# Another order of the same instructions in a fused attention kernel, and a load moved behind a transfer

## The reference

```python
# layer 0, per batch (c = 128 channels, n = 512 positions)
energy    = (w_qk y)^T (w_qk x)                    # 512 x 512
attention = softmax(energy, rows)
attention = attention / (1e-7 + attention.sum(over rows))
x_r = relu(w_t (x - (w_v x + b_v) attention) + b_t)
x2  = x + x_r
# layer 1, per batch: 128 rows of 512, 32 query heads on 8 key heads of width 16
q, k, v = x2 Wq + bq, y Wk + bk, y Wv + bv
out = softmax(q k^T / 4 + mask) v Wo + bo
out_x = layernorm(out + x2) * gamma + beta
```

## Time and profile before

| | |
|---|---|
| median of 3 runs | 779.62 us (779.21 to 782.26) |
| the profiled execution | 782.72 us, span 780.3 us |
| mean granted clock of TensorE | 0.980 |
| TensorE busy | 716.9 us (92%), weight loads 579.4 (74%) |
| VectorE busy | 608.3 us (78%) |
| GpSimd busy | 582.2 us (75%) |
| ScalarE busy | 463.5 us (59%) |
| HBM | 41.50 MB read, 8.39 MB written |

### The profile page before, as it was taken

One profiled execution on the slowest core, in us unless ns is written; L12 is line 12 of the kernel. 1 busy time (PEld: TensorE's weight loads), 2 busy tenths in 40 slices (PEclk: granted clock), 3 DMA queues, 4 the chain that ended last, 5 costly groups with the idle time before them and its releaser, 6 DMA issues.

```text
span 780.3 us, 17141 instructions
## 1 busy us (share of the span) xinstructions
PE 716.9 (92%) x4886; PEld 579.4 (74%) x4886; DVE 608.3 (78%) x1030; ACT 463.5 (59%) x1058; POOL 582.2 (75%) x752
## 2 busy tenths in 40 slices
PE   6798979999999999999999999999999999998773
PEld 5676867888788787878778787877878787775642
DVE  5675875969789796969879696978879697885747
ACT  5655638376574937657483855747385665748161
POOL 4886488697877969787896978789697878858054
PEclk9999999999999999999999999999999999999896
DMA  8544361634527262452717254362715436251511
GB/s 321 176 123 125 92 177 55 177 99 148 138 94 191 83 179 89 152 142 89 205 68 184 88 157 129 101 191 74 200 66 171 122 116 170 81 146 61 136 37 61
DMA packets 60363, 101.64 MB, mean 130 GB/s; under 512 B 10032, under 2 KB 30128, under 8 KB 60208
## 3 DMA queue, kind: packets, MB, share of 16 engines
q1 hardware_dynamic: 59616, 101.03, 43.6%
q10 hardware_dynamic: 720, 0.27, 0.2%
HBM read 41.50 MB, written 8.39 MB: 64 GB/s over the span
## 4 chain that ended last, share of the span: by engine, by line
PE 66%; DVE 12%; DMA 9%; issue 5%; SPq 3%; POOL 2%; ACT 1%; DVEq 1%; POOLq 0%; ACTq 0%
PE banks L924 8%; PE banks L840 7%; DMA qstack<-mrep 7%; DVE maxima L1567 6%; PE banks L937 5%; PE banks L871 4%; PE banks L873 4%; PE banks L872 4%; PE banks L895 4%; PE banks L827 2%; PE banks L825 2%; PE banks L826 2%; PE banks L813 2%; SPq L403 2%; PE banks L949 2%
## 5 line engine op out<-in xcount | busy, mean ns | idle before, releaser
L1567 DVE TENSOR_REDUCE maxima<-banks 128x4 f32<-128x512 f32 x256 | 158.9, 685 | 5.9 <-PE banks L895 4.5
L1226 ACT ACTIVATE prob<-banks 128x512 f32<-128x512 f32 x256 | 135.1, 608 | 26.3 <-PE banks L924 25.0
L1592 DVE RECIPROCAL dens<-dens 128x512 f32<-128x512 f32 x30 | 100.4, 3348 | 46.6 <-DMA dens<-sides 46.6
L601 POOL TENSOR_TENSOR ta<-ta,cb_s 128x516 f32<-128x516 f32 x64 | 77.1, 1205 | 74.9 <-ACT ta L1168 74.8
L840 PEld LDWEIGHTS banks<-ta,att 128*128 128x128 f32 x1024 | 119.0, 190 | 2.7 <-POOL ta L608 0.2
L840 PE MATMUL banks<-ta,att 128*128 128x130 f32 x1024 | 119.4, 275 | 0.0
L1160 ACT ACTIVATE att<-banks,negmax 128x512 f32<-128x512 f32 x128 | 88.7, 716 | 33.7 <-DVE negmax L1517 33.6
L1210 ACT ACTIVATE qh<-banks,bq_s 128x256 fp32r<-128x256 f32 x64 | 30.7, 480 | 104.1 <-PE banks L873 104.1
L924 PE MATMUL banks<-qstack,kstack 128*128 128x512 f32 x256 | 81.4, 422 | 9.5 <-DMA qstack<-mrep 9.2
L1517 DVE TENSOR_REDUCE negmax<-banks 128x1 f32<-128x512 f32 x128 | 85.2, 685 | 3.9 <-PE banks L827 3.7
L871 PE MATMUL banks<-x2h,wq_h 128*128 128x256 f32 x256 | 74.5, 291 | 4.1 <-POOL x2l L669 4.1
(11 more groups left out here) (170 smaller groups left out, 1956.1 us busy)
## 6 DMA issues: line engine op xcount, KB each, us to landing
qstack<-qh SPq DMA_DIRECT2D x128, 128.0 KB, 2.4
xs<-in_x SPq DMA_DIRECT2D x16, 512.0 KB, 4.4
ys<-in_ctx SPq DMA_DIRECT2D x16, 512.0 KB, 3.8
et<-in_ctx_turned SPq DMA_DIRECT2D x16, 512.0 KB, 3.3
xt<-in_x_turned SPq DMA_DIRECT2D x16, 512.0 KB, 3.6
kstack<-kph SPq DMA_DIRECT2D x128, 64.0 KB, 2.0
qstack<-ql SPq DMA_DIRECT2D x64, 128.0 KB, 2.4
out_x<-late SPq DMA_DIRECT2D x32, 256.0 KB, 2.1
```

Of the source, the lines that this page charges most:

```text
L601: nc.gpsimd.tensor_tensor(part, part, cb_s[:].unsqueeze(1).broadcast_to([P, 2, CW]), ALU.add).then_inc(sem["ta_done"], 1)
L1226: nc.scalar.activation(prob[:, 2 * p + odd], banks[:, slot(plan, f"st{j}{kv}")], exp_f).then_inc(sem["prob_done"], 1)
L1567: nc.vector.tensor_reduce(maxima[:, 0, :, p, :, g].rearrange("x o j -> x j o"), banks[:, slot(plan, f"mx{g}{p}")].rearrange("x (j o s) -> ...
L1592: nc.vector.reciprocal(dens[:], dens[:]).then_inc(sem["dinv_done"], 1)
```

## The change

Each engine's `iteration` gets another order of the same steps, and `WIDE_USES` the order that goes with TensorE's. Turn 0 and the work after turn 15 are as they were. The core of the diff:

```diff
 SyncE
                 if s2:
                     stack_q(q)
+                    stack_maxima(q)
                 if load_next:
                     next_y(i)
                 if s2:
-                    stack_maxima(q)
+                    gather_denominators(q, 0)
+                    gather_values(q, 0)
                 if load_next:
                     next_et(i)
                 if s2:
-                    gather_denominators(q, 0)
-                    gather_values(q, 0)
+                    gather_denominators(q, 1)
...
-                if s1:
-                    stack_k(i)
                 if s3:
                     store(i - 2, 1)
+                if s1:
+                    stack_k(i)
 GpSimd
                 if s1:
-                    scale_values(i, 0)
                     add_bias(i, 1, 0)
                     add_bias(i, 1, 1)
                 if split_next:
                     split_x(i + 1, 0)
+                if s1:
+                    scale_values(i, 0)
+                if split_next:
                     split_x(i + 1, 1)
                 if s3:
                     variance(i - 2)
                     newton_root(i - 2)
+                if s1:
+                    scale_values(i, 1)
...
                 if split_next:
                     split_y(i + 1, 0)
+                if s1:
+                    spread_k(i)
+                if s2:
+                    residual_bias(q, 0)
+                if split_next:
                     split_y(i + 1, 1)
-                if s1:
-                    scale_values(i, 1)
-                    spread_k(i)
-                if s2:
-                    residual_bias(q, 0)
 TensorE
                 if s1:
+                    energy(i, plan, 0, 0)
                     tva_project(i, plan, 0, 0)
-                    energy(i, plan, 0, 0)
                     energy(i, plan, 0, 1)
+                    tva_project(i, plan, 0, 1)
                     energy(i, plan, 0, 2)
                     energy(i, plan, 0, 3)
-                    energy(i, plan, 1, 0)
+                    tva_project(i, plan, 0, 2)
                 if s3:
                     out_project(i - 2, plan, i, 0)
                 if s1:
-                    tva_project(i, plan, 0, 1)
-                    tva_project(i, plan, 0, 2)
+                    energy(i, plan, 1, 0)
...
                     energy(i, plan, 1, 1)
-                    energy(i, plan, 1, 2)
-                if s2:
-                    max_spread(q, plan, i)
                 if s0:
                     z_project(i, plan, 0)
                 if s1:
+                    energy(i, plan, 1, 2)
+                if s2:
+                    max_spread(q, plan, i)
+                if s1:
                     energy(i, plan, 1, 3)
...
-                    scores(q, plan, i, 0, 7, masked)
                 if s0:
                     z_project(i, plan, 1)
                 if s2:
                     residual_transpose(q, plan, i, 0)
+                    scores(q, plan, i, 0, 7, masked)
                     values(q, plan, i, 0, 0)
                     values(q, plan, i, 0, 1)
+                if s1:
+                    kv_project(i, plan, "v", 1, "v_ps")
...
                     scores(q, plan, i, 1, 6, masked)
+                    scores(q, plan, i, 1, 7, masked)
+                if s1:
+                    v_transpose(i, plan)
+                if s2:
                     residual_transpose(q, plan, i, 1)
-                    scores(q, plan, i, 1, 7, masked)
                     values(q, plan, i, 1, 0)
                     values(q, plan, i, 1, 1)
-                if s1:
-                    v_transpose(i, plan)
 ScalarE
+                if s1:
+                    exp_energy(i, plan, 0, 0)
                 if s2:
                     x2_high(q, 1)
...
                 if s2:
                     q_high(q, plan, 2)
                 if s1:
                     tva_raw(i, plan, 1, 0)
...
                 if s3:
                     at_high(i - 2, 1)
...
+                if s2:
+                    keep_sums(q, plan, 0, 0)
                 if s0:
                     z_high(i, plan, 1)
                 if s2:
-                    keep_sums(q, plan, 0, 0)
                     keep_sums(q, plan, 0, 1)
...
+                    at_high(q, 0)
                     keep_sums(q, plan, 1, 0)
-                    at_high(q, 0)
                     keep_sums(q, plan, 1, 1)
 VectorE
+                if s2:
+                    max_rows(q, plan)
                 if s1:
                     energy_max(i, plan, 1, 1)
-                if s2:
-                    max_rows(q, plan)
+                    energy_max(i, plan, 1, 2)
+                if s0:
+                    z_low(i, plan, 0)
                 if s3:
                     root_guess(i - 2)
                 if s1:
-                    energy_max(i, plan, 1, 2)
                     energy_max(i, plan, 1, 3)
                     ctx_low(i)
-                if s0:
-                    z_low(i, plan, 0)
-                if s1:
                     row_inverse(i, 1)
```

More of the change, by code:

```diff
@@ L493, in iteration @@
                     next_mask(i)
+                if s3:
+                    store(i - 2, 0)
                 if s2:
                     gather_values(q, 1)
+                if s3:
+                    store(i - 2, 1)
                 if s1:
                     stack_k(i)
-                if s3:
-                    store(i - 2, 1)
             def first_iteration(i, load_next, s1, s2, s3, setup=False):
@@ L701, in iteration @@
                     newton_root(i - 2)
+                if s1:
+                    scale_values(i, 1)
+                if weights:
+                    out_weights_low()
                 if split_next:
                     split_y(i + 1, 0)
-                    split_y(i + 1, 1)
                 if s1:
-                    scale_values(i, 1)
                     spread_k(i)
@@ L709, in iteration @@
                     residual_bias(q, 0)
+                if split_next:
+                    split_y(i + 1, 1)
                 if s3:
@@ L995, in iteration @@
                     energy(i, plan, 1, 1)
+                if s0:
+                    z_project(i, plan, 0)
+                if s1:
                     energy(i, plan, 1, 2)
@@ L1270, in iteration @@
                 q = i - 1
+                if s1:
+                    exp_energy(i, plan, 0, 0)
                 if s2:
                     x2_high(q, 1)
-                if weights:
-                    out_weights_high()
                 if s1:
-                    exp_energy(i, plan, 0, 0)
+                    exp_energy(i, plan, 0, 1)
                     tva_raw(i, plan, 0, 0)
-                    exp_energy(i, plan, 0, 1)
                     exp_energy(i, plan, 0, 2)
+                    tva_raw(i, plan, 0, 1)
                     exp_energy(i, plan, 0, 3)
+                    exp_energy(i, plan, 1, 0)
                 if s2:
@@ L1296, in iteration @@
                     tva_raw(i, plan, 1, 0)
+                if weights:
+                    out_weights_high()
+                if s3:
+                    at_high(i - 2, 1)
+                if s1:
                     tva_raw(i, plan, 1, 1)
@@ L1306, in iteration @@
                 if s1:
+                    ctx_high(i)
                     exp_energy(i, plan, 1, 1)
@@ L1335, in iteration @@
                     exp_scores(q, plan, 1, 2)
+                if s3 and (s1 or s2):
+                    normalise(i - 2, 1)
+                if s2:
                     exp_scores(q, plan, 1, 3)
                     exp_scores(q, plan, 1, 4)
-                if s3 and (s1 or s2):
-                    normalise(i - 2, 1)
+                if s1:
+                    x2_high(i, 0)
                 if s2:
@@ L1343, in iteration @@
                     exp_scores(q, plan, 1, 7)
+                    at_high(q, 0)
                     keep_sums(q, plan, 1, 0)
-                    at_high(q, 0)
                     keep_sums(q, plan, 1, 1)
-                    residual(q, plan, 1)
                 if s1:
-                    x2_high(i, 0)
                     v_place(i, plan, 0)
                     v_place(i, plan, 1)
+                if s2:
+                    residual(q, plan, 1)
             def first_iteration(i, plan, s0, s1, s2, s3, setup=False, weights=False):
@@ L1681, in iteration @@
                     inverse_denominators(i - 2, 1)
-                    residual_add(i - 2, plan, 0)
                 if s1:
                     energy_max(i, plan, 1, 0)
+                    row_inverse(i, 0)
                 if s3:
+                    residual_add(i - 2, plan, 0)
                     weigh_out(i - 2, 1)
@@ L1688, in iteration @@
                     q_low(q, plan, 0)
-                if s1:
-                    row_inverse(i, 0)
                 if s3:
@@ L1694, in iteration @@
                     score_max(q, plan, 0, 0)
+                    q_low(q, plan, 1)
```

(1 more changed line is left out.)

13 lines of the change are left out of this document (removed), and 18 rows, old and new, of the table WIDE_USES.

## The result

| | before | after |
|---|---|---|
| median | 780.94 us (779.21 to 783.69, 4 runs) | 771.58 us (769.09 to 774.36, 4 runs) |
| profiled execution, span | 782.72, 780.3 us | 772.18, 770.3 us |
| granted clock | 0.980 | 0.978 |

The ratio is 0.988 (95% interval 0.983 to 0.993). The kernel is faster by 1.2%; the forecast was 765 in 757 to 778. The mechanism forecast for the repeated turn is there, a little smaller than priced, and one step outside it, in turn 1, costs what no sentence of the prediction had priced.

What follows compares the result with a forecast made beforehand. TensorE held 66% of the chain; GpSimd's loop was to bind next, at 44.20 a turn. 12 x 0.87 = 10.4, plus 1.0, 3.1 and 0.5, gave 15.0: 767.7 profiled, 765 as median, range 757 to 778.

Steps and rivals of the forecast that it cites:

- The spread, the copy and the transfer: Middle of the loop turn: spread without idle, maxima sent 0.56 sooner, attention product ending 1.24 before the present first score.
- the slower rival: Before the spread: z waits for the split of x if that comes more than 0.78 late; 784, chance 0.10.
- the two ends for the transfer: SyncE's transfer of the maxima: 2.48, the end taken, at cost 0, or 3.48 if y disturbs it, at cost 0.68.
- Behind the first score: After the first score: z's bank 0.13 gained, exponential wait 0.1, v about 0, residual copy about 0.14 late.
- the gain of 1.26 for TensorE alone: Loop turn: TensorE's own gain, turn 43.81; the rival that TensorE alone decides gave 760, chance 0.13.
- 0.13 gained: Fifth score in the loop turn: it no longer waits for z's bank, 0.13 a turn.
- GpSimd as the new bound: Loop turn: GpSimd's 27.02 + 17.15 + 0.03 makes 44.20, a gain of 0.87 a turn; chance 0.45.
- about 0.4: Before the first q product: TensorE's wait for GpSimd's low part of x, about 0.4 a turn.
- Turn 1: Before the loop: GpSimd has room, the score's wait goes and the maxima leave 0.6 sooner; gain 1.0.
- Turn 2: Before the loop: maxima sent without y ahead land 3 earlier for the score that waited 3.30; gain 3.1.
- The end: After turn 15: GpSimd's idle 0.51 for ScalarE's high part of the weighted values goes; gain 0.5.

Runs made afterwards that it cites:

- the removal of the first wait: Kernel before with only the maxima copied ahead of the row maximum and sent ahead of the load of y: 779.9 us, ratio 0.997, turn 45.11.
- that of the second: Kernel before with only z ahead of the last but one energy and the spread, and z's low part earlier on VectorE: 783.59 us, turn 45.33.
- all three mends: Changed kernel with the output weights' split back in its old place, the second residual bias late and the first output product late: 760.33 us, ratio 0.973.

## Why the prediction was right, and where not

*The spread, the copy and the transfer* came as forecast: from turn 4 to the loop's end z does not wait for the split of x (so the slower rival had no ground), the spread stands without idle, and the scores follow the attention product at once. Of the two ends for the transfer, 2.48 and 3.48, the choice of the lower was right by the packets (about 2.5), and the kernel with y ahead shows the upper (3.80). Outside that stretch z does wait, 0.49 in turn 3 and more in turn 1:

```profile
59.03 0.50 PE L805 MATMUL banks<-xh,gram_h 128*128 128x512 f32 x1 [1.61 <-POOL xl L571]
```

There it stands in place of a longer wait of the spread (2.18 before, 0.18 now), and the way from the first product to that spread is as long as before, 21.69 for 21.68.

*Behind the first score* the gain of 1.26 for TensorE alone is right: 45.07 - 1.26 = 43.81, and 43.76 was measured once GpSimd was out of the way. One term in it was read wrongly: "0.13 gained" for z's bank is what was left of that wait behind the wait for the maxima, not its price. Taken alone the removal of the first wait gives nothing (45.11) and so does that of the second (45.33). The sum held only because the change made both moves; in this the forecast was lucky.

*GpSimd as the new bound* was right, with 44.36 measured for 44.20. The size was off by 0.16: from the variance to the end of the low part of x2 it is 27.15 (358.69 + 1.31 - 332.85) for 27.02, and from the first q product to the variance 17.20 (332.85 - 315.65) for 17.15. Other operations are stretched than before, with nearly the same sum. The wait was forecast ahead of q and stands one step earlier, ahead of the first output product: 0.31 from start to start for "about 0.4". Two low parts bind within 0.1 of each other: on GpSimd their ends are 360.00 - 356.24 = 3.76 apart, on TensorE their readers 360.05 - 356.37 = 3.68. The prediction followed only the second, so it would have missed that moving the bias alone is worth just 0.14. Over 12 turns the sizes cost 10.4 - 8.7 = 1.7.

*Turn 1 is the step that failed*: "Turn 1: GpSimd has room; [...] gain 1.0". The row of the waiting score was read there, but the diff of turn 1 was not followed to its end (the diff ahead of the prediction does not show these lines). It moves the split of the output weights, 4.55 on GpSimd, onto the buffer that the exponentials want. GpSimd did have room (busy 26.82 of 45.05 from spread to spread before); what failed is the order. Here is the stretch from the spread of turn 1 to that of turn 2, in this order for the kernel before, the changed kernel, the one with the weights back, the one with bias and output product late, and the one with all three mends:

```profile
61.14:106.19 45.05, 43.37 (x306) 35.31 (x306) 33.83 (x59) 26.43 (x63) 26.82 (x24) 1.00 0.41 116
60.87:108.99 48.12, 44.72 (x305) 36.11 (x306) 34.82 (x59) 26.48 (x64) 30.76 (x25) 0.96 0.40 115
65.63:110.60 44.97, 44.61 (x307) 36.64 (x306) 34.85 (x59) 26.92 (x65) 26.56 (x24) 0.96 0.39 116
63.04:110.71 47.67, 43.53 (x305) 35.10 (x306) 34.83 (x59) 26.00 (x64) 30.50 (x24) 1.00 0.38 112
61.47:104.93 43.46, 43.10 (x305) 35.29 (x306) 34.79 (x59) 26.36 (x64) 26.09 (x23) 1.00 0.41 120
```

The last number but two is the granted clock; the first behind the comma is how long TensorE was busy. The late split costs 48.12 - 44.97 = 3.15 at a clock of 0.96 and 47.67 - 43.46 = 4.21 at 1.00; within each of these pairs the code differs in nothing else. TensorE stands still 1.68, 3.40, 0.36, 4.14 and 0.36. So the waits that were priced at 1.0 were worth 1.68 - 0.36 = 1.32, and the split added 3.40 - 0.36 = 3.04. The other 44.72 - 43.37 = 1.35 that the changed kernel lost is busy time: TensorE's granted clock fell to 0.50 at 71.33, when it had just stood still those 3.04. With the weights back it fell to 0.50 at 65.52, behind a wait of 1.97, so that kernel's profile does not show the 1.0. The last one, at 1.00, does: 45.05 - 43.46 = 1.59, in which the loop's two mends may have a share.

Together turn 1 lost 3.1 where 1.0 was to be won. These 4.1 are the largest part of what the span fell short: the loop lacks 1.7 and the end 0.9, while turn 2's stretch and the start give 1.7 more than summed, which leaves the 5.0. In these differences TensorE's clock stands with 1.35 lost in turn 1, about 1.3 won in turn 2 and, as the rows below show, 1 to 2 lost at the end.

*Turn 2* gave what was said. The transfer is issued at 110.45 and the score that waited 3.30 waits for nothing:

```profile
113.37 1.40 PE L927 MATMUL banks<-qstack,kstack 128*128 128x512 f32 x5
```

Its stretch won 4.53. TensorE's idle time fell there by 3.19, from 4.07 to 0.88, which is the 3.1; its busy time fell by 1.34, and with it goes the granted clock, 0.97 before and 1.00 now. So the 0.9 of a turn's gain cannot be read from this stretch.

*The end* lost 0.41 in this execution, where 0.5 was to be won. The next q product does come sooner after spread 15 (24.60 for 26.11, and its wait falls from 4.14 to 2.91), but from q to the next spread 19.24 pass and not 17.50. That is the clock and none of the moves. Three of the other kernels have the same instructions from spread 15 on: the one with the weights back, the one with y ahead (turn 15 loads no y) and the one with z's low part late (turn 15 makes no z). The stretch from q to the next spread, in the kernel before, the changed one and those three:

```profile
722.66:740.16 17.50, 13.99 (x92) 11.77 (x92) 13.93 (x25) 2.14 (x5) 0.00 (x0) 0.82 0.61 150
710.74:729.98 19.24, 16.21 (x92) 14.04 (x93) 14.87 (x25) 1.90 (x4) 0.00 (x0) 0.68 0.57 140
712.95:731.16 18.21, 15.32 (x92) 13.06 (x93) 14.81 (x25) 1.90 (x4) 0.00 (x0) 0.72 0.60 147
730.19:749.08 18.89, 14.97 (x92) 12.80 (x92) 14.87 (x25) 2.53 (x5) 0.03 (x1) 0.75 0.58 142
726.33:743.90 17.57, 14.05 (x93) 11.84 (x93) 14.83 (x25) 2.15 (x5) 0.00 (x0) 0.81 0.62 152
```

The same products keep TensorE busy 16.21, 15.32, 14.97 and 14.05 as the granted clock goes from 0.68 over 0.72 and 0.75 to 0.81. From spread 15 to the end the four take 84.13, 83.06, 81.92 and 82.37, the kernel before 83.72. So the changed kernel's own profile is the slowest of the four, and the others win 0.7 to 1.8 where 0.5 was forecast.

The median fell by 9.4, the span by 10.0. Turn 1 began anywhere from 39.2 to 43.9 in the profiled executions of these kernels, whose code up to there is the same. Where it began by 40.4, the clock granted from 13 us to there was 0.99 or 1.00; where it began later, it was 0.86 to 0.94. A single execution is off by as much as half the gain, so the argument rests on turn lengths in the loop and on medians, and on stretches outside it only at a like clock.

## What to carry to other kernels

A wait's price is not the number in its brackets when a second wait ends beside it: before a wait is priced, ask what each of the next instructions would wait for if it were gone, and test the two removals together. Follow the diff through the first and last passes of a loop as well, where steps stand that the loop never shows, and for each moved step look at the buffer that it borrows. When one engine becomes the bound, list every product that it hands over in a turn; two of them may be due within a tenth of a microsecond. Before a stretch outside the loop is compared between two executions, read the clock granted in each.

## What the runs showed of the hardware

A transfer of 64 KB took 3.80 us when issued behind a load of 512 KB; with no other edit made, its last packet ended 2.22 us after the issue when it was issued 0.76 ahead of that load. The first matmul after a stop of TensorE took 0.49 where its neighbours take 0.40. After waits of TensorE of 2 to 3 us outside the loop, its granted clock was 0.50 for some microseconds in some executions and not in others: the same products kept it busy 16.21 us at a mean of 0.68 and 14.05 at 0.81. The start of turn 1 differs by 4.7 us between the profiled executions, half of what the change is worth.
